# Layer norm, cross attention and a block-quantised FFN on one core: the FFN written out pair by pair, with three gate and up banks and twelve inner slots

## What is computed

```python
x = x + _L0_xattn_ref(_layernorm(x), ctx_2048, Wq, Wk, Wv, Wo)
x = x + _L0_ffn_ref(_layernorm(x), w_gate, w_up, w_down)

# the FFN; _q_act: blocks of 32 along the row share an exponent, floor(log2(amax));
# each element is rounded to 3 fraction bits and clipped to 7.5 of its block's unit
gate = einsum("bsh,oh->bso", _q_act(x), _q_w(w_gate))      # 512 -> 2048
up = einsum("bsh,oh->bso", _q_act(x), _q_w(w_up))
inter = silu(gate) * up
return einsum("bsh,oh->bso", _q_act(inter), _q_w(w_down))  # 2048 -> 512
```

## Time and profile before

| | us |
|---|---|
| median of 3 runs (2052.83 to 2056.01) | 2053.23 |
| profiled execution, its time | 2054.62 |
| its span | 2053.1 |
| PE busy in the span | 2019.0 (98%) |
| DVE busy | 1534.7 (75%) |
| ACT busy | 999.6 (49%) |
| POOL busy | 739.8 (36%) |

### The profile page before, as it was taken

The page is one execution under the profiler, slowest core; times in us unless marked ns, Lnnn a source line. Parts: engine busy times, 40 slices in busy tenths (PEclk is TensorE's granted clock), DMA queues, the critical chain, the costliest instruction groups (busy, mean ns, idle before and its releaser), DMA issues. The chain is left out here.

```text
span 2053.1 us, 45755 instructions
## 1 busy us (share of the span) xinstructions
PE 2019.0 (98%) x15430; PEld 1503.3 (73%) x15430; DVE 1534.7 (75%) x3339; ACT 999.6 (49%) x2683; POOL 739.8 (36%) x882
## 2 busy tenths in 40 slices
PE   8999999999999999999999999999999999999997
PEld 6888878788888887878888888888888874444443
DVE  6767777877777777777777777775666558888886
ACT  8955555445555454555555555555555452223222
POOL 5422232323233233323333333231111006777776
PEclk9999999999999999999999999999999999999999
DMA  8834444444445444444444445443333273454554
GB/s 256 212 72 84 86 93 84 93 88 88 88 89 91 91 91 85 89 91 91 91 87 88 87 91 88 91 86 75 68 67 70 55 173 79 79 87 87 89 87 79
DMA packets 455038, 193.26 MB, mean 94 GB/s; under 512 B 418400, under 2 KB 431200, under 8 KB 454848
## 3 DMA queue, kind: packets, MB, share of 16 engines
q1 hardware_dynamic: 432496, 139.26, 35.2%
q0 software_dynamic: 16016, 45.23, 9.3%
q10 hardware_dynamic: 6336, 6.29, 1.0%
HBM read 61.21 MB, written 27.26 MB: 43 GB/s over the span
## 5 line engine op out<-in xcount | busy, mean ns | idle before, releaser
L1094 PE MATMUL b_qk<-kvT,attn_weights 128*128 128x256 f16 x3072 | 377.2, 273 | 3.7 <-DVE qk L763 2.9
L1094 PE MATMUL b_qk<-xT,attn_weights 128*128 128x256 f16 x3072 | 377.2, 273 | 0.0
L1094 PE MATMUL b_v<-attn_weights,kvT 128*128 128x256 f16 x3072 | 377.2, 273 | 0.0
L654 ACT ACTIVATE prob<-b_s,nmax 128x256 f32<-128x256 f32 x514 | 238.8, 469 | 278.2 <-DVE nmax L924 276.4
L1094 PEld LDWEIGHTS b_qk<-kvT,attn_weights 128*128 128x128 f16 x3072 | 299.9, 98 | 93.2 <-issue 5.1
L951 DVE SCALAR_TENSOR_TENSOR psplit<-prob,rrec,psplit 128x256 f16<-128x256 f32 x514 | 306.0, 636 | 79.5 <-ACT psplit L664 79.5
L763 DVE SCALAR_TENSOR_TENSOR qk<-b_qk,qk 128x512 f16<-128x512 f32 x256 | 176.5, 690 | 246.6 <-ACT qk L610 236.1
L610 ACT ACTIVATE qk<-b_qk 128x512 f16<-128x512 f32 x256 | 152.4, 595 | 425.2 <-PE b_qk L1094 424.9
L1094 PEld LDWEIGHTS b_v<-attn_weights,kvT 128*128 128x128 f16 x3072 | 300.2, 98 | 35.1
L1094 PEld LDWEIGHTS b_qk<-xT,attn_weights 128*128 128x128 f16 x3072 | 300.2, 98 | 35.1
L664 ACT ACTIVATE psplit<-prob,rrec 128x256 f16<-128x256 f32 x514 | 233.1, 500 | 68.1 <-DVE rrec L944 68.1
(11 more groups left out here) (132 smaller groups left out, 2635.7 us busy)
## 6 DMA issues: line engine op xcount, KB each, us to landing
ffn_w<-wffn SPq DMA_DIRECT2D x48, 256.0 KB, 2.8
acc<-xtok POOLq DMA_DIRECT2D x16, 512.0 KB, 4.9
out<-acc POOLq DMA_DIRECT2D x16, 512.0 KB, 3.3
xrow<-xtok POOLq DMA_DIRECT2D x31, 256.0 KB, 3.2
out<-attn_weights POOLq DMA_DIRECT2D x31, 256.0 KB, 4.5
kvrow<-kvt POOLq DMA_DIRECT2D x61, 128.0 KB, 2.4
stage<-wattn SPq DMA_DIRECT2D x12, 512.0 KB, 4.4
ffn_scratch<-ffn_t SPq DMA_DIRECT2D x48, 128.0 KB, 2.4
```

What stands on the lines that cost most here:

```text
L654: last = eng.activation(half(prob, q, 256), half(bS, q, 256), ACT.Exp, bias=nmax[:, q:q + 1], scale=1.0, accum_out=rsum[:, q:q + 1])
L1094: last = eng.matmul(out, l, r, start=(a == 0), stop=(a == len(pairs) - 1))
```

## The change

It changes the FFN alone.

1. **Banks.** The scores and context banks of the attention become a third gate and a third up bank. From slice 4 on, slice `u` waits for `inner` of slice `u - 3` (`GU_BUF`, `GU_FREE`).
2. **Slots.** The transposed pairs get twelve slots instead of four. `NO_DOWN` names the pairs at which PE does no `down`: 0 to 3, 36, 40, 44, 48 and 52. So `down` lags 4 pairs behind from pair 4 on, and 9 pairs from pair 53 on; after the last `gate_up` PE has `down` 55 to 63 left (`BEHIND`).
3. **Order on DVE.** Both `inner`, `reduce`, `clip` of the pair before, the scales, `round_a`.
4. **Order on POOL.** `round_b` of the pair, then `rescale` of the pair before, then a step of `POOL_STEPS`, then `add_out`.
5. **Order on ACT.** `silu`, `scale` of the pair before, `silu`, `move_down`; the block scales have two buffers.
6. **End.** The last pair is transposed by SP's DMA; PE's transposes and the copies back are gone. The last two tiles are added by DVE and stored by SP; `add_out` is left for tiles 0 to 29.
7. **Straight code** for all 64 pairs on every engine. An identity matrix in BF16 and its two POOL instructions at the start are gone.

SP's order is as before: the transpose of the even pair, then the load of tile `t + 2`.

```diff
+INNER_SLOTS = 12
+NO_DOWN = (0, 1, 2, 3, 36, 40, 44, 48, 52)
+DOWN_AT = {v: d for d, v in enumerate(v for v in range(PAIRS) if v not in NO_DOWN)}
+MOVE_AT = {v: d // 2 for v, d in DOWN_AT.items() if d % 2}
+BEHIND = range(len(DOWN_AT), PAIRS)
+GU_BUF = [u % 2 if u < 4 else (u - 2) % 3 for u in range(2 * PAIRS)]
+GU_FREE = [max([w + 1 for w in range(u) if GU_BUF[w] == GU_BUF[u]], default=0) for u in range(2 * PAIRS)]
...
-        gate = [bPT, bQK]
-        up = [bX, bV]
+        gate = [bPT, bQK, bS]
+        up = [bX, bV, bC]
...
@@ sync @@
+            for v in range(PAIRS):
+                transpose_inner(v)
+                if v % 2 == 0 and v // 2 + 2 < TILES:
+                    load_x_tile(v // 2 + 2, v // 2 % 2)
...
@@ gpsimd @@
-                    if not (isinstance(v, int) and v == 0):
-                        rescale(v - 1, 1 - h)
-                    round_b(v, h)
...
+            def pair(v):
+                round_b(v, v % 2)
+                if v > 0:
+                    rescale(v - 1, (v - 1) % 2)
...
+                if v - 1 in MOVE_AT:
+                    add_out(MOVE_AT[v - 1], MOVE_AT[v - 1] % 2)
...
@@ scalar @@
+            for v in range(PAIRS):
+                for k in range(2 * (v % 2), 2 * (v % 2) + 2):
+                    if v > 0:
+                        silu(v // 2, k)
+                    if v > 0 and k % 2 == 0:
+                        scale(v - 1)
+                if v in MOVE_AT:
+                    move_down(MOVE_AT[v], MOVE_AT[v] % 2)
+            scale(PAIRS - 1)
+            for t in range(TILES - 2):
+                if 2 * t + 1 in BEHIND:
+                    move_down(t, t % 2)
...
@@ vector @@
+            def pair(v):
+                t, h = v // 2, v % 2
+                if v > 0:
+                    inner(t, 2 * h)
+                    inner(t, 2 * h + 1)
+                reduce(v, h)
+                if v > 0:
+                    clip(v - 1)
+                scales(v)
+                round_a(v, h)
...
+                if v in LAST_STEPS:
+                    last_step(*LAST_STEPS[v])
...
+            eng.wait_ge(sm["down_done"], PAIRS - 2)
+            eng.wait_ge(sm["x1_stored"], 16 * B)
+            eng.tensor_tensor(last_rows[0], o_bank[0][:, :], last_rows[0], ALU.add).then_inc(sm["last_added"], 1)
             eng.wait_ge(sm["down_done"], PAIRS)
-            eng.tensor_tensor(last_rows, o_bank[1][:, :], last_rows, ALU.add).then_inc(sm["last_added"], 1)
+            eng.tensor_tensor(last_rows[1], o_bank[1][:, :], last_rows[1], ALU.add).then_inc(sm["last_added"], 1)
...
@@ tensor @@
+            for v in range(PAIRS):
+                for u in range(2 * v, 2 * v + 2):
+                    if u >= 3:
+                        gate_up(u // 4, u % 4, u // 4 % 2)
+                if v in DOWN_AT:
+                    down(DOWN_AT[v])
+            for d in BEHIND:
+                down(d)
```

More of the change, by code:

```diff
@@ L568, in add_out @@
                               accum_op=ALU.add).then_inc(sm[f"out_stored{at}"], 16)
-            def tile(t, at, out_=True, last_batch=False):
-                for h in range(2):
-                    v = 2 * t + h
-                    if not (isinstance(v, int) and v == 0):
-                        rescale(v - 1, 1 - h)
-                    round_b(v, h)
[L576 to L596, removed]
+            def pair(v):
+                round_b(v, v % 2)
+                if v > 0:
+                    rescale(v - 1, (v - 1) % 2)
+                if v == 0:
+                    store_x1(B - 1, acc[:, 0:2 * D].rearrange("p (t d) -> p t d", t=2))
+                step = POOL_STEPS.get(v)
+                if step == "rstd":
+                    tile_rstd(B - 1)
+                for j in range(2):
+                    if step == f"round{j}":
+                        x_round(TILES - 2 + j, j)
+                    if step == f"rescale{j}":
+                        x_rescale(TILES - 2 + j)
+                if v == 4:
+                    eng.wait_ge(sm["x1_stored"], 16 * B)
+                if v - 1 in MOVE_AT:
+                    add_out(MOVE_AT[v - 1], MOVE_AT[v - 1] % 2)
+            for v in range(PAIRS):
+                pair(v)
             wait_apart(eng, "i_clip", PAIRS)
@@ L599, in _ @@
             q = half(iq, 2)
[L600 to L603, removed]
+            eng.tensor_tensor(by_block(q), by_block(q), spread(i_scale[:, 32:32 + NBLK]), ALU.mult).then_inc(sm["i_q"], 1)
+            for t in range(TILES - 2):
+                if t not in [MOVE_AT.get(v - 1) for v in range(PAIRS)]:
+                    add_out(t, t % 2)
         @block.scalar
@@ L731, in scale @@
                 eng.wait_ge(sm["i_pow_done"], v + 1)
[L732 to L754, removed]
+                if v >= 2:
+                    eng.wait_ge(sm["i_q"], v - 1)
+                eng.activation(half(i_scale, v % 2, 32), i_pow, ACT.Copy, scale=16.0).then_inc(sm["i_scale_done"], 1)
+            for v in range(PAIRS):
[7 more added lines that the diff above has]
+            scale(PAIRS - 1)
+            for t in range(TILES - 2):
+                if 2 * t + 1 in BEHIND:
+                    move_down(t, t % 2)
         @block.vector
         def _(eng):
-            eng.wait_ge(sm["ident_ready"], 6)
+            eng.wait_ge(sm["ident_ready"], 4)
             def lo(dst, src, hi_part, scale, ready, value, done):
```

169 lines of the change are left out of this document (59 added, 110 removed).

## The result

The changed kernel takes 2063.9 us where the kernel before took 2053.0 beside it: a ratio of 1.0053, with a 95% interval of 1.0041 to 1.0065, so 0.5% slower. Two of its six runs, left out here, took 7357 and 8108 us (in the one with a profile a 256 column product took 693 ns instead of 273), and so the profile after is that of the same kernel run once more (2063.7 us, ratio 1.0050, interval 1.0033 to 1.0067), whose span is 2061.6 us.

What follows compares the result with a forecast made beforehand. TensorE was taken as the bound, with 8.7 us of bank waits. 1715.5 + 300.4 + 5.3 + 14.5 + 20.0 put its end at 2055.7, 9.5 later than before; added to 2053.2 this gave 2062.7 us, range 2050 to 2070.

Steps and rivals of the forecast that it cites:

- pair 4 starts: Start of the FFN: TensorE begins pair 4 at 1715.5, when tile 2's load lands; the kernel before begins it at 1713.71.
- TensorE's own time to the last gate and up: From pair 4 to the last gate and up product: 309.1 us less five put-off `down` (8.6), so 300.4.
- waits behind steps of the last batch: Pairs 10, 14, 16, 20 and 24: last-batch steps delay `rescale`, so TensorE waits 5.3 us in all.
- waits at pairs 34 to 62: TensorE waits for x tiles: 11.5 us where a `down` is left out, 3.0 for loads at pairs 54 and 58; 14.5 us.
- ten `down` at the end: After the last gate and up product: 17.3 us of `down` and a 2.6 us bank wait, 20.0 in all.
- from there to the end of the span: Behind TensorE's last product: one addition and one store, claimed to take as long as before, 6.9 us.
- The path of the x tile: From g, the end of an odd pair's products: load at 9.1, landed at 12.0, or 13.6 beside the DMA.
- rival by which nothing changes: X tile's path: 0.3 us shorter and the DMA costs it nothing, so about 2055 us; chance 0.20.
- The rival by which the tile is in time: X tile's path is about 10.4 us, not 12.0, so no leave-out is eaten: 10 us less, 2043; chance 0.10.
- VectorE as the bound: FFN pairs: VectorE or the DMA engines become the bound, slower still, 2075 us; chance 0.08.
- The DMA's price: X load beside GpSimd's accumulating DMA: landing 4.3 us instead of 2.6; the 1.6 extra could be 1.0 by the queue rule.
- What costs nothing: FFN: ACT's order, third bank (`inner` 2 us ahead), straight code; end's transpose hidden by `down` 55 to 61, otherwise 3 us.

Runs made afterwards that it cites:

- the moved waits: Kernel before with GpSimd's last waits, for the two last accumulating DMAs, moved to SyncE: 2052.9 us, ratio 0.9993.
- three buffers: Changed kernel with the x load ahead of the transpose, plus three instead of two buffers for the sums of `down`: 2038.6 us, ratio 0.9928.

## Why the prediction was right, and where its steps were off

The forecast was 2062.7 us, and the kernel takes 2063.7 to 2063.9. Of the medians the loss is 10.7 us, of the profiled spans 8.5 (the profiled execution before was 1.4 us above its median); 9.5 was forecast. The mechanism is the one forecast: the 8.7 us of bank waits go, and more comes back as waits for the x tile. The steps, on TensorE, in us:

| step | forecast | measured |
|---|---|---|
| pair 4 starts | 1715.5 | 1715.30 |
| TensorE's own time to the last gate and up | 300.4 | 303.3 |
| lower clock behind three waits | none | 5.1 |
| waits behind steps of the last batch | 5.3 | 2.4 |
| waits at pairs 34 to 62 | 14.5 | 12.4 |
| ten `down` at the end | 20.0 | 19.2 |
| TensorE ends | 2055.7 | 2057.65 |
| from there to the end of the span | 6.9 | 4.0 |

(From pair 4 to the last gate and up product 2038.45 - 1715.30 = 323.15 us pass; less the listed waits, 14.8, and the clock's 5.1, 303.3 are left.)

- *The path of the x tile* holds: load at g + 8.9 (9.1 and 0.13 forecast), TensorE ready at g + 10.5 (10.36), landing 4.1 beside the DMA (4.3). The load stands at g + 8.9 in the same way for pairs 38, 46, 50, 54, 58 and 62. The forecast's links add up to 11.8 and 13.5 us and not to the 12.0 and 13.6 that it used, and the measured path is shorter by a further 0.2: so half of the rival by which nothing changes came true, and its other half, that the DMA costs the load nothing, did not. The rival by which the tile is in time is out, and so is VectorE as the bound: the load first shows both, since it takes the waits away and leaves VectorE's work as it is.
- *Which pairs.* Pair 4 4.64; pair 38 1.15 (1.7 forecast), 42 2.52 (3.2), 46 2.16 (1.7), 50 3.04 (3.2), 54 1.07 (1.7), 58 and 60 2.0 together (3.0 forecast), and 0.45 at pair 36, where none was forecast. At pair 46 the landing took 3.8 us and not 2.6, though no DMA of GpSimd was issued beside it; the last one before it was 6.8 us earlier. It takes 3.7 with `add_out` at even pairs too, so `add_out` doesn't make it. Four other loads of the change took 3.3 to 3.9 us with no such DMA issued from 5 us before them to 3 us behind, among them the one for pair 38 (3.3). What makes them long is not shown.
- *Steps of the last batch* were sized twice too large. The waits are 0.46 at pair 16, 1.36 at pair 20 and 0.58 at pair 22; the 1.3 for `tile_rstd` and the 1.9 for `x_rescale` didn't show. I had added each instruction's length as if VectorE and GpSimd had no slack there; which part of it the slack took, no run separates.
- *The lower clock* is the term that was missing. I had priced a wait at its length; three of them cost 1.7 us more each.
- *TensorE's own time* was sized right, though 303.3 stands against 300.4. A listed wait begins at the modelled end of the product before, 0.16 us behind the point at which the next product could start: from 1914.48 to 1918.89 are 4.41 us, the eight products' 1.73, the 2.52 listed and 0.16 more. Eleven such waits behind pair 4 make 1.8. Three gaps of 0.3 (behind the `down` of 1735.99, 1842.84 and 1863.87), each of which ends as an x tile lands, are not listed and make 0.9. This leaves 300.6. With the load first it is 301.1 (1710.49 to 2013.66, less 2.1 of waits), of which 0.6 is of the same kind. So the 2.9 us are waits for the x tile as well, and the x waits sum to 22.2 us (with the 0.16 at pair 4) and not to 19.4.
- *The end* is as forecast: one wait for the bank, 1.6 instead of 2.6. `add_out` of tile 26 was issued 7.2 us behind the last gate and up product and not 7.7, and landed in 4.1 us and not in 4.5; and the forecast's own terms (7.7, 4.5 and 0.6, less 10.4) make 2.4.
- *What comes behind* was said to be as before, and was 2.9 us shorter. Neither straight code (a wait of 4.1 us for TensorE's sequencer at the very end, 3.7 in the kernel before) nor the moved waits (0.7 us, but 2.0 with the load first in the kernel before, which doesn't touch the end) make a time that can be told apart. The length of this wait differs between kernels without a cause that I found; it stays open. With three buffers it took nearly what the shorter end had brought.

So misses of 8.0 us upwards (5.1 for the clock, 2.9 of unlisted x waits) and of 8.9 downwards (0.2, 2.9, 2.1, 0.8 and 2.9) nearly cancel on the span, 2061.6 against 2062.6; the forecast's size owes that to luck, its sign and its place don't. *The DMA's price* came out as the trace has it and not as the 1.0 of the prediction's estimate: the landings for pairs 42 and 50 were 4.1 and 4.6 against 2.6 without it (1.5 and 2.0 more). *What costs nothing* held in the main: three banks bring 6.0 us, though with the load first two waits for `inner` (2.1 us) are left, so `inner` isn't done 2 us ahead everywhere; straight code brings nothing; and the end's transposes, which the put-off `down` hide, cost 6.8 us without them and not the 3 I gave.

The best kernel here is the change with the x load ahead of the transpose: 2038.4 us, 0.7% below the kernel before.

## What to carry to other kernels

When an instruction is moved behind another one, follow everything that is queued behind its consumer: here `rescale` gates a transpose, and an unrelated load stood behind that transpose on SyncE's queue, which cost 25 us until the load was issued first. Work that is taken off the bounding engine in the middle only pays if nothing else is due then: the same five put-off `down` cost 9.7 us beside a late tile and brought 5.2 without it. And price a wait of TensorE that is as long as those that brought the lower clock here (2.15 to 4.64 us, though not each of them did) at its length and what the clock may add, 1.7 us here.

## What the runs showed of the hardware that I had not expected

- *TensorE's clock.* Behind waits of 4.64, 2.16 and 3.04 us the granted clock fell to the 1.2 GHz level for two groups of four products or somewhat more, and each time 1.7 us were lost; behind 2.52 us it stayed at 2.4 GHz. In the kernel with GpSimd's old order it stayed there behind 2.79 us too (the next group follows 0.87 us later), and of three waits of 2.15 us there it fell behind one (0.66 of full speed from 1940 to 1945). So the length of the wait alone doesn't decide it. With all `down` in their place, the last `down`, behind waits of 2.88, 2.14 and 1.79 us, took 3.59 us instead of 1.90, at a granted clock of 0.50.
- *VectorE held by GpSimd, in a steady state.* 0.69 us of `round_a` become 2.25 beside a `rescale`, in the mean over 53 pairs, and the kernel loses 34 us. The profile counts the time held as busy.
- *The accumulating DMA beside a transposing load* costs the load 1.5 and 2.0 us at pairs 42 and 50 (4.1 and 4.6, against 2.6 each without it). The three late ones at the end took 4.6, 5.0 and 4.0.
